# The last token group's normed rows transposed by VectorE from rows that went through memory, its gate logits in quarters of the array, and another order of the first group's weight splits

## What is computed

```
xn  = layernorm(x)                                   # 4096 x 256
x1  = x + attn0(xn) + ffn0(xn)                       # layer 0: chunked attention, 16 gated experts
xn1 = layernorm(x1)
gate_logits = xn1 @ gate_W        (256 x 4)          # which 2 of 4 scans, and their weights
gate_logits = xn1 @ gate_w.T + b  (256 x 8)          # which of 8 experts (argmax)
out = x1 + mix of 4 gated linear scans over xn1 (sigmoid, tanh, sigmoid) + chosen expert's MLP(xn1)
```

## Time and profile before

| | |
|---|---|
| median of 3 runs | 1003.04 (1002.76 to 1003.16) |
| the profiled execution's own time | 1003.55 |
| its span, first to last instruction | 1001.9 |
| TensorE busy | 995.2 (99%) |
| VectorE busy | 791.6 (79%) |
| ScalarE busy | 625.3 (62%) |
| GpSimd busy | 395.0 (39%) |
| DMA, mean | 155 GB/s |

### The profile page before, as it was taken

How to read it: one execution, slowest core, us unless ns; L and a number is a source line. 1 busy time by engine, 2 the same in 40 slices (tenths; PEclk the granted TensorE clock), 3 DMA queues, 4 the chain that set the end, 5 groups by cost and what they waited for, 6 DMA issues and landing times.

```text
span 1001.9 us, 21041 instructions
## 1 busy us (share of the span) xinstructions
PE 995.2 (99%) x6834; PEld 894.1 (89%) x6834; DVE 791.6 (79%) x1359; ACT 625.3 (62%) x1198; POOL 395.0 (39%) x393
## 2 busy tenths in 40 slices
PE   8999999999999999999999999999999999999998
PEld 7888988989899898988888888999999999888887
DVE  6876777667686777979789898987788777688897
ACT  4554545545454454555566667988889898566665
POOL 3444444444444444443563864122122210266400
PEclk9999999999999999999999999999999999999999
DMA  6227313122132231452574376689888887645913
GB/s 192 74 69 240 109 42 84 43 83 84 42 84 84 74 94 43 136 200 65 183 262 167 128 250 236 200 272 291 276 260 272 279 266 233 225 136 135 201 43 42
DMA packets 121124, 155.32 MB, mean 155 GB/s; under 512 B 49200, under 2 KB 89136, under 8 KB 120048
## 3 DMA queue, kind: packets, MB, share of 16 engines
q1 hardware_dynamic: 100912, 133.42, 41.0%
q0 software_dynamic: 14464, 15.61, 6.9%
q10 hardware_dynamic: 5696, 5.64, 1.7%
HBM read 110.26 MB, written 44.37 MB: 154 GB/s over the span
## 4 chain that ended last, share of the span: by engine, by line
PE 99%; DMA 1%; DVE 0%; ACT 0%; issue 0%; DVEq 0%; SPq 0%
PE ps L396 19%; PE ps L398 19%; PE ps L397 19%; PE ps L1235 6%; PE ps L1236 6%; PE ps L1237 6%; PE ps L1652 4%; PE ps L1651 4%; PE ps L1653 4%; PE ps L1635 2%; PE ps L1254 2%; PE ps L1253 2%; PE ps L1255 2%; PE ps L1306 1%; DMA stage<-keys 1%; PE ps L1298 1%
## 5 line engine op out<-in xcount | busy, mean ns | idle before, releaser
L865 POOL TENSOR_TENSOR acc<-acc,ytmp 128x512 f32<-128x512 f32 x120 | 159.0, 1325 | 230.2 <-ACT ytmp L955 214.2
L1691 ACT ACTIVATE act_o<-ps,scan_bias 128x512 f32<-128x512 f32 x189 | 129.6, 688 | 92.2 <-PE ps L398 87.9
L955 ACT ACTIVATE ytmp<-ps,sel 128x256 f32<-128x256 f32 x256 | 107.3, 471 | 94.6 <-PE ps L1237 94.0
L1235 PE MATMUL ps<-vals_h,hT_h 128*128 128x256 f32 x512 | 144.6, 282 | 0.3 <-issue 0.2
L1032 DVE SCALAR_TENSOR_TENSOR hT_l<-ps,hT_h 128x512 fp32r<-128x512 f32 (+1 forms) x136 | 88.3, 655 | 71.5 <-ACT hT_h L915 71.3
L1236 PE MATMUL ps<-vals_l,hT_h 128*128 128x256 f32 x512 | 143.8, 281 | 0.0
L1237 PE MATMUL ps<-vals_h,hT_l 128*128 128x256 f32 x512 | 143.5, 280 | 0.0
L915 ACT ACTIVATE hT_h<-ps 128x512 fp32r<-128x512 f32 x128 | 76.4, 597 | 80.3 <-PE ps L398 75.5
L1888 POOL DMA_DIRECT2D rows<-xs_d x92 | 52.8, 575 | 169.4 <-DVE sT L2139 154.4
L1077 DVE SCALAR_TENSOR_TENSOR acc<-ps,sel,acc 128x256 f32<-128x256 f32 x240 | 104.0, 474 | 3.0 <-PE ps L1237 2.8
L1235 PEld LDWEIGHTS ps<-vals_h,hT_h 128*128 128x128 f32 x512 | 96.4, 188 | 7.0 <-issue 1.9
(11 more groups left out here) (265 smaller groups left out, 2768.0 us busy)
## 6 DMA issues: line engine op xcount, KB each, us to landing
raw<-w SPq DMA_DIRECT2D x78, 512.0 KB, 5.3
x1T<-xT_d SPq DMA_DIRECT2D x16, 512.0 KB, 5.6
comb_b<-comb_d SPq DMA_DIRECT2D x8, 1024.0 KB, 7.6
w_small<-w SPq DMA_DIRECT2D x16, 512.0 KB, 5.3
xn_d<-xn SPq DMA_DIRECT2D x15, 512.0 KB, 3.0
xs_d<-zeros ACTq DMA_DIRECT2D x1, 4992.0 KB, 20.4
x_d<-x SPq DMA_DIRECT2D x8, 512.0 KB, 4.4
xT_d<-nT_h SPq DMA_DIRECT2D x8, 512.0 KB, 2.7
```

The source lines that it names most:

```text
L865: pool.tensor_tensor(dst[:, 2:4, :], acc[:, 2:4, :], ytmp[:, k % 2, :, :], ALU.add).then_inc(acc23, 1)
L955: act.activation(ytmp[:, k % 2, j - 2, :], yb(k, j), ACT.Copy, scale=sel[:, j, k:k + 1]).then_inc(y_23, 1)
L1235: pe.matmul(yb(k, j), hT_h[:, k % 2, s], vals_h[:, k, :], start=True, stop=False)
L1691: act.activation(act_o[:, i % 2, w, :], ps[:, 3 * (i % 2) + w, :], func, bias=scan_bias[:, w, i:i + 1]).then_inc(act_g, 1)
```

## The change

It has four parts.

1. **Rows through memory.** `post_transposes` goes. SP waits for the stores of x1 and xn1 of group 7 and loads `nq` in four quarters before `xT1_store`. VectorE turns them (`turn_n`) at i = 2 into `last_nT`, which is the memory of xn1. ScalarE makes `nT_h` from it at i = 3, VectorE `nT_l` at i = 3. SP's wait for the three stores in front of `body(0)` becomes a wait for two in front of the quarter loads; the wait for the third moves behind `lg_ok`.
2. **Logits in quarters.** `last_logits` is now the 8 float32 matmuls of `post_logits` (`gate_products`), and waits for `turn_n`. One ScalarE copy takes them out.
3. **`gw` and its two instructions go**; TensorE waits for `small_in` in place of `gw_ready`. `x1` and `xn1` change places with `nT_h` and `nT_l` in memory.
4. **Split order of the first group:** vals2 from k = 4 to 5, o from 5 to 6, keys3 from 6 to 8.

```diff
-    gw = ra("gw", [P, DC, P // Q32, Q32], F32R)
...
-    x1 = ra("x1", [P, JT, D], F32)
-    xn1 = ra("xn1", [P, JT, D], F32)
     nT_h = ra("nT_h", [P, DC, GT], F32R)
     nT_l = ra("nT_l", [P, DC, GT], F32R)
+    xn1 = ra("xn1", [P, JT, D], F32)
+    x1 = ra("x1", [P, JT, D], F32)
+    last_nT = xn1[:].rearrange("p (c j) d -> p c (j d)", c=DC)
...
-    def last_logits_T(act, g):
...
+    def turn_n(dve, g, dst):
+        dve.wait_ge(nq_in, 16 * N_Q * (g + 1))
+        for c in range(DC):
+            dve.transpose(dst[:, c, :].rearrange("p (h r) -> p h r", r=Q32), nq[:, :, turned_part(c)]).then_inc(n_turned, 1)
...
-    def post_transposes(pe, g):
-        pe.wait_ge(xn1s, JT * (g + 1))
-        pe.wait_ge(side_free, freed(g, "lg"))
-        pe.wait_ge(mix_free, 1)
...
+    def gate_products(pe, turned):
         for c in range(DC):
+            tokens = turned[:, c, :].rearrange("p (j t) -> p j t", j=JT)
             for q in range(P // Q32):
                 quarter = slice(q * Q32, (q + 1) * Q32)
                 last_mm = pe.matmul(ps[quarter, 6, 0:P], gw_raw[:, c, :], tokens[:, :, quarter], start=c == 0, stop=c == DC - 1)
         last_mm.then_inc(side_full, 1)
-    def last_logits(pe, g):
-        pe.wait_ge(side_free, post_use(g, "t1")[2])
-        for c in range(DC):
-            gate = gw[:, c].rearrange("p q n -> p (q n)")
-            pe.matmul(ps[:, 6, :], gate, nT_h[:, c, :], start=c == 0, stop=False)
-            last_mm = pe.matmul(ps[:, 6, :], gate, nT_l[:, c, :], start=False, stop=c == DC - 1)
...
+    def last_logits(pe):
+        pe.wait_ge(n_turned, DC * GROUPS)
+        pe.wait_ge(side_free, freed(GROUPS - 1, "lg"))
+        gate_products(pe, last_nT)
...
     def xT1_store(sp, g):
-        if isinstance(g, int) and g == GROUPS - 1:
-            sp.wait_ge(side_free, post_use(g, "t1")[2])
-        else:
-            wait_alone(sp, nT_ok, DC * (g + 1))
+        wait_alone(sp, nT_ok, DC * (g + 1))
...
-        FIRST_SPLITS = {0: ["g"], 1: ["keys1"], 2: ["vals1"], 3: ["keys2"], 4: ["vals2"], 5: ["o"],
-                        6: ["keys3"], 10: ["vals3"]}
+        FIRST_SPLITS = {0: ["g"], 1: ["keys1"], 2: ["vals1"], 3: ["keys2"], 5: ["vals2"], 6: ["o"],
+                        8: ["keys3"], 10: ["vals3"]}
...
             x1_store(sp, g)
             xn1_store(sp, g)
-            xT1_store(sp, g)
             sp.wait_ge(x1_st, 16 * GROUPS)
             sp.wait_ge(xn1_st, 1 + 16 * GROUPS)
-            sp.wait_ge(xT1_st, 1 + 32 * GROUPS)
+            for b in range(N_Q):
+                sp.dma_start(nq[b * Q32:(b + 1) * Q32], xn1_q[g, b]).then_inc(nq_in, 16)
+            xT1_store(sp, g)
             sp.wait_ge(side_full, post_use(GROUPS - 1, "lg")[0] + 1)
             body(0)
             sp.wait_ge(lg_ok, GROUPS)
+            sp.wait_ge(xT1_st, 1 + 32 * GROUPS)
...
                     scan_products(pe, g, i)
-                    if zero(g) and i == 2:
-                        post_transposes(pe, GROUPS - 1)
                     if zero(g) and i == 4:
-                        last_logits(pe, GROUPS - 1)
+                        last_logits(pe)
...
                 step(0, i)
-                if i == 2:
+                if i == 3:
                     act.wait_ge(xT1_st, 1 + 32 * g)
-                    t_hi(act, post_use(g, "t1")[0], nT_h[:], side2)
+                    act.wait_ge(n_turned, DC * GROUPS)
+                    act.activation(nT_h[:], last_nT, ACT.Copy).then_inc(nT_hi_ok, 1)
                 if i == 4:
-                    last_logits_T(act, g)
+                    logits_T(act, g)
...
                 if i == 2:
-                    lo_of(dve, post_use(g, "t1")[1], nT_l[:], nT_h[:], side2)
+                    turn_n(dve, g, last_nT)
+                if i == 3:
+                    dve.wait_ge(nT_hi_ok, GROUPS)
+                    dve.tensor_tensor(nT_l[:], last_nT, nT_h[:].bitcast(F32), ALU.subtract).then_inc(nT_ok, DC)
```

More of the change, by code:

```diff
@@ L329, in build @@
     small_in = sem("small_in")
[L330 to L331 removed]
+    e_bias = sem("e_bias")
+    lg_turned, lg_ok = sem("lg_turned"), sem("lg_ok")
     consts = sem("consts")
@@ L461, in gate_logits @@
     def gate_logits(dve, g):
-        if isinstance(g, int) and g == GROUPS - 1:
-            dve.wait_ge(lg_T, P // Q32 - 1)
-        dve.wait_ge(side_free, post_use(g, "lg")[2])
+        dve.wait_ge(side_free, post_use(g, "lg")[1])
         dve.transpose(lg_rows[:].rearrange("p j n -> p (j n)"), lgT[:].rearrange("p j t -> p (j t)")).then_inc(lg_turned, 1)
         dve.wait_ge(lg_turned, g + 2)
[L467 to L471, removed]
+        dve.tensor_copy(logits[:, bass.ds(g * JT, JT), :], lg_rows[:, :, 0:NL]).then_inc(lg_ok, 1)
+    def turn_n(dve, g, dst):
+        dve.wait_ge(nq_in, 16 * N_Q * (g + 1))
+        for c in range(DC):
+            dve.transpose(dst[:, c, :].rearrange("p (h r) -> p h r", r=Q32), nq[:, :, turned_part(c)]).then_inc(n_turned, 1)
     def turned_part(c):
@@ L506, in post_logits @@
         last_mm.then_inc(side_full, 1)
-    def last_logits(pe, g):
-        pe.wait_ge(side_free, post_use(g, "t1")[2])
-        for c in range(DC):
-            gate = gw[:, c].rearrange("p q n -> p (q n)")
-            pe.matmul(ps[:, 6, :], gate, nT_h[:, c, :], start=c == 0, stop=False)
-            last_mm = pe.matmul(ps[:, 6, :], gate, nT_l[:, c, :], start=False, stop=c == DC - 1)
-        last_mm.then_inc(side_full, 1)
+    def post_logits(pe, g):
+        pe.wait_ge(n_turned, DC * (g + 1))
+        pe.wait_ge(o_gate, g + 2)
+        gate_products(pe, xT)
+    def last_logits(pe):
+        pe.wait_ge(n_turned, DC * GROUPS)
+        pe.wait_ge(side_free, freed(GROUPS - 1, "lg"))
+        gate_products(pe, last_nT)
     def mixture_rank(dve, link, mx, j):
@@ L1111, in body @@
                     if k == 7 and not first:
-                        dve.wait_ge(nq_in, 16 * N_Q * g)
-                        for c in range(DC):
-                            dve.transpose(xT[:, c, :].rearrange("p (h r) -> p h r", r=Q32), nq[:, :, turned_part(c)]).then_inc(n_turned, 1)
+                        turn_n(dve, g - 1, xT)
                     if k in (8, 9):
@@ L1147, in body @@
                     if k == 5 and first:
-                        dve.wait_ge(gw_ready, 1)
-                        gate = gw_raw[:, :, 0:NL].unsqueeze(2).to_broadcast((P, DC, P // Q32, NL))
-                        dve.tensor_tensor(gw[:, :, :, NL:2 * NL], gate, gw[:, :, :, 0:NL].bitcast(F32), ALU.subtract).then_inc(gw_ready, 1)
+                        dve.wait_ge(small_in, 16 * 4)
                         dve.tensor_tensor(ebias[:], ebias[:], gate_b[:], ALU.add).then_inc(e_bias, 1)
@@ L1338, in _ @@
             body(0, True, False)
-            pe.wait_ge(gw_ready, 2)
+            pe.wait_ge(small_in, 16 * 4)
             with pe.Fori(1, GROUPS - 2) as g:
@@ L2296 @@
         "scan_bias": c(turned(np.stack([i["L1_attn_bg"], i["L1_attn_bv"], i["L1_attn_bd"]]), 2).reshape(3, MC, P).transpose(2, 0, 1)),
-        "gates": c(turned(np.concatenate([i["L1_attn_gate_W"], i["L1_ffn_gate_w"].T] * 2 + [np.zeros((D, Q32 - 2 * NL), np.float32)], axis=1), 0)),
+        "gates": c(turned(np.concatenate([i["L1_attn_gate_W"], i["L1_ffn_gate_w"].T, np.zeros((D, Q32 - NL), np.float32)], axis=1), 0)),
         "gate_b": c(i["L1_ffn_gate_b"]),
```

16 lines of the change are left out of this document (3 added, 13 removed).

## The result

The changed kernel takes 1005.90 (median of 9 runs, 1004.84 to 1006.50) against 1003.04 (9 runs, 1002.67 to 1004.21): a ratio of 1.0027, 95% interval [1.0019, 1.0035]. It is slower, by some 2.9. The profiled execution took 1005.98, 2.43 more than the profiled one of before (1003.55); its span is 1004.3.

A forecast was written before the change was run, and what follows sets the result against it. TensorE was taken as the bound, with 99% of the chain at full clock. Saved work, stall, refill, second wait and split order, -1.11 + 2.9 + 0.1 + 0.2 + 0.15 = +2.3 on 1003.04, gave 1005.3, range 1003.2 to 1007.4.

The forecast's parts named there:

- Work saved and the wait for the turned rows: Last group's gate matmuls on TensorE: 1.11 of work saved, then a stall of 2.9 (bounds 2.2 to 4.4) for `n_turned`.
- the chain of four links: Path of the turned rows: xn1 store lands 510.4, quarter loads 515.3, VectorE's transposes end 516.6, TensorE needs them at 513.8.
- The second wait: Scan group 1's turned rows load behind the late split-half stores; TensorE waits 0.2 for them, bounds 0 to 1.4, or 2.3.
- the subtraction ending past 523: Sign of being right: VectorE's new subtraction, behind its long queue, ends at 523.1 to 524.0, where it used to end at 510.7.
- Other edits at nothing: Single copies, the `small_in` wait and the memory exchange cost nothing; r_hot comes about 531 against a need at 534, cover 3.
- Who queues behind the waits: Engines behind the turned rows: ScalarE and GpSimd cost nothing; VectorE's long queue delays the new subtraction to 523.1 to 524.0.
- The split order: First group of stage A: holes move, don't close; the matmul at 57.91 comes 0.15 later, bounds 0.3 later to 0.9 earlier.
- a first group that ends its step 10 earlier than 57.9: Sign of being wrong, in stage A's first group, where 0.15 later was forecast for the matmul at 57.91.
- The clock: Rival: TensorE's clock falls in the stall, a step of 4.2 takes 8.4, giving 1009.5; chance 0.05.

The follow-up runs named there:

- the first trace: The changed kernel as made, its first profiled execution: 1005.98, against 1003.55 for the profiled execution of the kernel before.
- the experiment: New split order alone in the kernel before: 1003.23, ratio 1.0000; old split order put back into the changed kernel: 1005.60, ratio 1.0024.
- The trace with the old order: Traced execution of the changed kernel with the old split order of the first group put back; median 1005.60, ratio 1.0024.
- the two other kernels with early stores: Changed kernel with stores ahead of the late weights, plus old split order: 1002.89, 0.9997; or plus weighting behind the second low half: 1003.22, 0.9999.

## Why the prediction was right or wrong

The forecast was 1005.3, the range 1003.2 to 1007.4; measured 1005.9. Its main mechanism held, one term was missing, and a rival's chance was set far too small. That the number came so near is in part luck: the missing 1.2 and 0.1 to 0.2 too little for the wait stand against 0.3 too much for the first group, 0.1 that the changed kernel gains in the rest of stage A and 0.25 that it regains behind the first slot.

- **Work saved and the wait for the turned rows.** Forecast 2.9, measured 3.2 in the first trace; the store landed after 10.2 where before had 9.8, and the chain of four links is otherwise as forecast: loads at 510.15 (510.5), the last landing ends VectorE's wait at 515.01 (515.3), transposes 1.30. Removing the cause gave back 3.7 of the time.
- **The second wait.** Forecast 0.2, measured 0.13 and 0.11 in the matmul behind, but by two errors that cancel. The sign "the subtraction ending past 523" failed: it ended at 521.82, since the choice of experts, priced at 3.32, took 1.5 (its first two operations 0.35 and 0.39, where in before they took 1.15 and 1.37 while GpSimd was at work). The loads went out at 522.88, not 524.7. Against that, TensorE had the rows 7.9 after the end of the subtraction, not 7.1 (530.2 less 523.1), near the upper bound in which they queue fully behind the stores (8.3). The subtraction took 1.21, as of old and in every trace of the changed kernel. I had priced a collision with GpSimd at up to 0.9, by the weighting's rows. GpSimd was there, but started later and was the one to wait:

```profile
520.76 2.21 POOL L1801 TENSOR_TENSOR accO<-accO,hw_b 128x512 f32<-128x512 f32 x1 [0.62 <-DVE hw_b L2055]
...
529.65 1.29 POOL L1801 TENSOR_TENSOR accO<-accO,hw_b 128x512 f32<-128x512 f32 x1
```

  It took 2.21 against 1.29 for the same operation later, and VectorE's scan behind the subtraction then took 2.32 in place of 1.28. This agrees with the rule of the Trainium skill (SBUF — State Buffer, SBUF: two separate sides) that the two take whole turns and that the one which starts first keeps its own: the subtraction started 0.15 ahead of GpSimd's operation.
- **The missing term: "Other edits at nothing" and "Who queues behind the waits".** I followed VectorE's queue behind the new wait only to the load of scan group 1's rows and to the one-hot (cover 3 by my sum; it ended at 532.9 against 534.0, so 1.1). I didn't ask where VectorE would find 6.3 of idle time to catch up. Up to the first expert slot it finds a part, arrives 2.9 late, and has not as much to spare: 1.2 lost there in the changed kernel, 2.3 in the kernel before with VectorE alone delayed.
- **The split order.** The term, +0.15, was for the new order with the `gw` instructions gone. Measured: order +0.09, removal -0.22, so -0.13. The holes went where I had put them, one closed at 52.1, one new in front of `down(10)` at 54.46. The error is the instructions that I held to lie wholly beside TensorE's work (a conclusion, see the experiment). By the letter a sign of being wrong was met here, "a first group that ends its step 10 earlier than 57.9": it was 57.38. But 0.53 of that was there by 18 us, from a start-up that varies between executions, so of the change itself nothing is left at that point. The sign should have been read against the group's start.
- **The clock.** I gave the fall 0.05, because no row of before showed one; but no row of before had a wait of 3 in mid-kernel either. It happened in 12 of 17 runs. Its price was 2.5 in this kernel's trace and 1.5 to 1.6 in three others, not 4.2, and VectorE's lateness in the first slot covers 1.2 of it. It adds 0.2 between the medians of the runs with and without it.

Sum by the measured terms of the first trace: 2.25 in the last group's stretch, 1.2 in the first slot, -0.13 in the first group, -0.1 in the rest of stage A, -0.25 regained in later slots, -0.5 from a start-up that varies between executions of every kernel here: 2.5, against 2.43 between the two profiled executions. Without that start-up, which is not the change's, it is 3.0, against 2.86 between the medians.

What stays open: why the store lands after 8.8 in one execution and 10.7 in another (8.4 to 9.8 in the four traces of before and its variants), and the spread of the kernels with early stores (1001.6 to 1004.8). The trace with the old order (1007.76) shows one more source of spread: 1.0 was lost near 760, in a later slot, behind a weight load for which ScalarE waited 1.1. The change with its stores moved ahead of the late weights has the lowest median, 1002.2, 3.7 below the change as it was made. That it is faster than the kernel before is not shown: its own interval only just excludes 1 (0.999 [0.9981, 0.9999]), and those of the two other kernels with early stores don't.

## What to carry to other kernels

Ahead of a trip through memory on a shared queue, look at what lies in front of the store, not only at the store's size: 1.5 MB of weights that nobody needed for another ten microseconds decided this change. When an engine that is not the bound gets a wait, follow its queue until its idle time has made up for it, however far, and at each point where the bound needs it compare the lateness of the two: what counts is how much later it is than the bound, less what it had to spare. Here that point was 130 us on. And a wait of TensorE's of 3 us in mid-kernel should be priced with a stretch at half clock as a likely case, even where the old trace has none.

## What the runs showed of the hardware

After a wait of 3.2 to 3.3 of TensorE the granted clock fell to 0.50 in some executions and stayed at 1.00 in others of the same kernel; with 13 matmuls in the wait it fell in none of 6. The fall was seen also behind a wait of 2.7 and one of 2.2, and behind one of 3.6. It cost 1.5 to 2.5. A small linked copy of 128x128 on VectorE took 0.38 in one kernel (9.79 for 26) and 0.45 in another (7.14 for 16).
